# Four layers of attention and feed-forward on one core: attention and the feed-forward of the item two behind interleaved, the experts' outputs scaled by ScalarE and added by GpSimd

## The reference

```python
x = x + xattn0(ln(x))   # 16 heads of 8, key mask, 64 learned memory keys/values
x = x + ffn0(ln(x))     # 128 -> 512, exact GELU, -> 128, plus a rank-style term
                        # built from tokens 1..16 of each item, scaled
x = x + xattn1(ln(x))   # 16 heads, rms norm of q and k
x = x + ffn1(ln(x))     # 4 experts 128 -> 512 -> 128, silu(x@w1)*(x@w3) @ w2,
                        # the best 2 of each token weighted by the gates
x = x + xattn2(ln(x))   # 16 heads, rotary embedding
x = x + ffn2(ln(x))     # 8 experts (352 wide), top 2, plus a shared one (176)
x = x + xattn3(ln(x))   # one head of 128
x = x + ffn3(ln(x))     # top-2 weights of 7 gates times one matrix, plus shared
```

## Time and profile before

| | us |
|---|---|
| median of 3 runs | 1201.09 (1197.25 to 1201.25) |
| profiled execution: its own time | 1206.52 |
| its span | 1204.7 |
| busy: PE, PEld, DVE, ACT, POOL | 1005.4, 656.7, 552.0, 440.4, 261.5 |
| mean granted clock | 0.762 |

### The profile page before, as it was taken

One profiled execution on the slowest core, in us unless ns is written; L12 is line 12 of the kernel. 1 busy time (PEld: TensorE's weight loads), 2 busy tenths in 40 slices (PEclk: granted clock), 3 DMA queues, 4 the chain that ended last, 5 costly groups with the idle time before them and its releaser, 6 DMA issues. The chain is left out here.

```text
span 1204.7 us, 14263 instructions
## 1 busy us (share of the span) xinstructions
PE 1005.4 (83%) x5034; PEld 656.7 (55%) x5034; DVE 552.0 (46%) x1203; ACT 440.4 (37%) x649; POOL 261.5 (22%) x375
## 2 busy tenths in 40 slices
PE   3788777858658888779999788788789999999986
PEld 3534333225534444338888563433348888888874
DVE  2644453313344454424554544454434454534458
ACT  2344443332205434452343225444442332322240
POOL 7201032214314442211110104241110010101044
PEclk9666675567766555568999995655579999999997
DMA  5001010110001101110000002201210000000001
GB/s 126 2 1 19 1 19 2 18 18 16 1 0 54 37 1 36 36 18 9 1 1 1 1 13 64 43 14 35 40 21 5 1 1 1 1 1 1 1 1 35
DMA packets 24715, 21.01 MB, mean 17 GB/s; under 512 B 6559, under 2 KB 19847, under 8 KB 24519
## 3 DMA queue, kind: packets, MB, share of 16 engines
q1 hardware_dynamic: 24647, 20.10, 7.8%
HBM read 12.33 MB, written 1.05 MB: 11 GB/s over the span
## 5 line engine op out<-in xcount | busy, mean ns | idle before, releaser
L1134 DVE TENSOR_REDUCE mneg<-PS 128x4 f32<-128x624 f32 (+1 forms) x192 | 170.7, 894 | 180.5 <-PE PS L751 180.2
L1546 ACT ACTIVATE work<-PS 104x1024 f32<-104x1024 f32 (+1 forms) x160 | 163.5, 1022 | 182.4 <-PE PS L833 180.6
L1286 DVE TENSOR_TENSOR work<-PS,work 128x512 f32<-128x512 f32 (+2 forms) x168 | 114.8, 685 | 211.4 <-PE PS L885 134.9
L1576 ACT ACTIVATE work<-PS 128x512 f32<-128x512 f32 (+2 forms) x168 | 99.9, 597 | 243.5 <-PE PS L885 241.5
L902 PEld LDWEIGHTS PS<-down_w,work 128*128 128x128 f32 (+2 forms) x1472 | 175.4, 194 | 6.2 <-DVE work L1286 1.0
L902 PE MATMUL PS<-down_w,work 128*128 128x128 f32 (+2 forms) x1472 | 175.9, 277 | 0.7 <-DVE work L1286 0.7
L883 PE MATMUL PS<-xh_sb,arena 128*128 128x512 f32 (+2 forms) x352 | 152.6, 433 | 9.5 <-DVE work L1286 9.2
L848 PE MATMUL PS<-work,vb_sb 104*32 104x512 f32 (+1 forms) x640 | 147.6, 1014 | 3.4 <-ACT work L1546 3.4
L885 PE MATMUL PS<-xh_sb,arena 128*128 128x512 f32 (+2 forms) x352 | 142.8, 406 | 0.0
L884 PE MATMUL PS<-xl_sb,arena 128*128 128x512 f32 (+2 forms) x352 | 142.4, 405 | 0.0
L751 PE MATMUL PS<-kb_sb,qxt_sb 49*128 49x312 f32 x256 | 69.5, 530 | 57.9 <-DVE mneg L1134 52.7
(11 more groups left out here) (165 smaller groups left out, 1164.7 us busy)
## 6 DMA issues: line engine op xcount, KB each, us to landing
v_den<-raw_sb SPq DMA_DIRECT2D x24, 256.0 KB, 5.0
stage<-in_w SPq DMA_DIRECT2D x8, 256.0 KB, 5.2
stage<-in_wg SPq DMA_DIRECT2D x8, 176.0 KB, 2.5
stage<-in_wu SPq DMA_DIRECT2D x8, 176.0 KB, 2.5
x_res<-in_x SPq DMA_DIRECT2D x4, 256.0 KB, 4.9
down_w<-in_w SPq DMA_DIRECT2D x1, 1024.0 KB
down_w<-in_wd SPq DMA_DIRECT2D x8, 128.0 KB
out<-x_res SPq DMA_DIRECT2D x4, 256.0 KB, 2.3
```

What stands on the lines that cost most here:

```text
L1134: dve.tensor_reduce(to, PS[:, bank:bank + 2, 0:HB * head_width(layer)].rearrange("p f (n h) -> p f h n", h=HB), AX.X, ALU.max, negate=True ...
L1286: dve.tensor_tensor(HH[0:rows, e % 2, j, :], PS[0:rows, 2 * (n % 2) + 1, :], SS[0:rows, n % 2, :], ALU.mult).then_inc(*sig["h"].mark((i, n)))
L1546: act.activation(P[0:rows, m % P_RING, :, :], PS[0:rows, 0:2, :], ACT.Exp, scale=SCALE).then_inc(*sig["p"].mark((i, m)))
L1576: act.activation(SS[0:rows, n % 2, :], PS[0:rows, bank, :], ACT.Silu).then_inc(*sig["act"].mark((i, n)))
```

## The change

The items no longer run one after the other. The program is 15 steps. Step s does attention item s (0 to 11, layers 0 to 2) and feed-forward item s - 2, the one whose attention was done two steps before; from step 12 on layer 3 takes the place of attention. `step_pieces` gives each piece of a step a position, sorts them, and all engines walk the sorted list: PE does `st`, `pv`, `up`, `down`, ACT the exps, tanh and scaling, and so on. Rings for x are per kind, `work` holds only the probabilities and a new `hidden` the hidden features, so that both kinds can run at once. Weights of layer 2 go where those of layer 1 are no longer needed, expert by expert.

The PSUM banks are dealt out anew: scores 0 and 1; maxima, transposes and all small products 2 and 3; values 4 (so an attention item is done in two halves of its heads, each evacuated to `raw_sb` by itself); gate and up 5 and 6; down 7.

Silu is computed as x (1 + tanh(x/2)) / 2: ACT takes the tanh, DVE adds 1 and multiplies by the gate bank, and multiplies by the up bank and 0.5. The sum over experts changes for all but the last expert of an item: ACT copies the down bank with the gate as scale into `lora_tmp`, four times 128 x 128, and GpSimd adds it to x.

```diff
+N_ATT = 3 * B
+SKEW = 2
+N_STEPS = N_ATT + SKEW + 1
+BANK_MX, BANK_PV, BANK_UP, BANK_Y, BANK_F3 = 2, 4, 5, 7, 0
...
+def ffn_item(f):
+    return (f // B) * 8 + B + f % B
...
+def attention_pieces(a, put):
+
+    i = item_of(a)
+    N, C = n_slots(i), quads(i)
+    W = width(a)
+    scale = W / 29.0
+    for m in range(N // 2):
+        put(2 * m, "st", i, m)
+    for u in range(2 * C):
+        put(4 * u + 5, "pv", i, u)
+    put(4 * C + 2.5, "evac", i, 0)
+    put(N + 3, "evac", i, 1)
...
+def ffn_pieces(f, W, put):
+
+    i = ffn_item(f)
+    kind = ITEMS[i][0]
+    tiles = ffn_tiles(kind)
+    if kind == "F0":
+        for n in range(4):
+            put(1.7 + 2.2 * n, "up", i, n, 0)
+        put(W * 0.45, "down", i, 0)
+        put(W * 0.45 + 1, "acc", i, 0)
+        return
+    for n in range(len(tiles)):
+        put(W * (n + 0.3) / len(tiles), "up", i, n, 0)
+        put(W * (n + 0.55) / len(tiles), "silu", i, n)
+        put(W * (n + 0.8) / len(tiles), "up", i, n, 1)
+    for e in range(tiles[-1][0] + 1):
+        last = max(n for n, tl in enumerate(tiles) if tl[0] == e)
+        x = W * (last + 2.1) / len(tiles)
+        put(x, "down", i, e)
+        put(x + 0.3, "acc", i, e)
...
+def step_pieces(s):
+
+    placed = []
+
+    def put(x, *piece):
+        placed.append((x, len(placed), piece))
+
+    W = width(s)
...
+    if s < N_ATT:
+        attention_pieces(s, put)
+    if SKEW <= s < N_ATT + SKEW:
+        ffn_pieces(s - SKEW, W, put)
...
+    if s == 12:
+        attention3_pieces(0, 0.8, put)
+        ffn3_pieces(0, 23.6, 30.0, put)
+    if s == 13:
+        attention3_pieces(1, 0.8, put)
+        attention3_pieces(2, 9.0, put)
+        ffn3_pieces(1, 9.9, 17.0, put)
+        ffn3_pieces(2, 18.0, 25.0, put)
+    if s == 14:
+        attention3_pieces(3, 0.8, put)
+        ffn3_pieces(3, 9.0, 16.0, put)
...
+                bank = BANK_UP + (kt % 2 if kind == "F0" else 0)
...
+                taken[bank + m] = sig["h_gelu" if kind == "F0" else "h" if m else "silu"].at((i, kt))
...
+                taken[BANK_Y] = accumulated(i, e)
...
+            def silu(i, n):
+                rows = ffn_tiles(ITEMS[i][0])[n][2]
+                dve.wait_ge(*sig["act"].at((i, n)))
+                dve.scalar_tensor_tensor(SS[0:rows, n % 2, :], SS[0:rows, n % 2, :], 1.0, PS[0:rows, BANK_UP, :],
+                                         ALU.add, ALU.mult).then_inc(*sig["silu"].mark((i, n)))
...
-                    dve.tensor_tensor(HH[0:rows, e % 2, j, :], PS[0:rows, 2 * (n % 2) + 1, :], SS[0:rows, n % 2, :], ALU.mult).then_inc(*sig["h"].mark((i, n)))
...
+                dve.scalar_tensor_tensor(HH[0:rows, e % 2, j, :], SS[0:rows, n % 2, :], 0.5, PS[0:rows, BANK_UP + 1, :],
+                                         ALU.mult, ALU.mult).then_inc(*sig["h"].mark((i, n)))
...
+                if e < last_expert(kind):
+                    return
...
-                    act.activation(SS[0:rows, n % 2, :], PS[0:rows, bank, :], ACT.Silu).then_inc(*sig["act"].mark((i, n)))
...
+                    act.activation(SS[0:rows, n % 2, :], PS[0:rows, BANK_UP, :], ACT.Tanh, scale=0.5).then_inc(*sig["act"].mark((i, n)))
...
+            def gated(i, e):
+
+                if e < last_expert(ITEMS[i][0]):
+                    act.wait_ge(*sig["y"].at((i, e)))
+                    if e == 0:
+                        act.wait_ge(*sig["gates"].at(i))
+                    if e > 0:
+                        act.wait_ge(*sig["acc"].at((i, e - 1)))
+                    elif ITEMS[prev_item(i)][0] == "F0":
+                        act.wait_ge(*sig["lora_l"].at(prev_item(i)))
+                    else:
+                        act.wait_ge(*sig["acc"].at((prev_item(i), last_expert(ITEMS[prev_item(i)][0]) - 1)))
+                    for t in range(T):
+                        ins = act.activation(YG[:, t * 128:(t + 1) * 128], PS[:, BANK_Y, t * 128:(t + 1) * 128], ACT.Copy,
+                                             scale=gates[:, gate_slot(i), t, e:e + 1])
+                    ins.then_inc(*sig["gated"].mark((i, e)))
...
+            def accumulate(i, e):
+
+                if e < last_expert(ITEMS[i][0]):
+                    b = ITEMS[i][2]
+                    if e == 0:
+                        pool.wait_ge(*sig["xn"].at(i))
+                    else:
+                        pool.wait_ge(*sig["acc"].at((i, e - 1)))
+                    pool.wait_ge(*sig["gated"].at((i, e)))
+                    xb = x[:, b * T:(b + 1) * T, :]
+                    pool.tensor_tensor(xb, YG[:, :].rearrange("p (t n) -> p t n", t=T), xb, ALU.add).then_inc(*sig["acc"].mark((i, e)))
...
```

1058 lines of the change are left out of this document (523 added, 535 removed).

## The result

The changed kernel takes 1300.9 us (median, 1299.2 to 1306.5) beside 1199.2 of the kernel before in the same comparison: a ratio of 1.086 (95% interval 1.081 to 1.090). It is slower by 102 us where the forecast said 145 us faster; 1301 is outside the range of 985 to 1130.

What follows compares the result with a forecast made beforehand. Attention was taken as limited by PE at half clock, F1 and F2 by PE at full clock, F0 and the tail by waits. Step terms summed to a 1060 us span, 1056 us measured time; 8-in-10 range 985 to 1130.

Steps and rivals of the forecast that it cites:

- The clock: Steps 6 to 13: TensorE was taken to hold the upper level, 2.4 GHz; the forecast's condition.
- The paragraph on banks: Gate, up and small products on single pairs: use of 38 or 42 us lies under a step's 68.
- 0 to 12, I take 57: Steps 0 and 1, attention alone: A0's 52.8 us plus 0 to 12 for shared banks 2 and 3, taken as 57.
- The table loads in them: Steps 2 to 5: 32 loads of 1.28 us around Gelu, mostly hidden, 4 us a step exposed.
- The work: Steps 6 to 13: 512 us of busy time times clock, put at 616 us, a rate of 0.83.
- The 2.4 us: Gate bank's cycle: matmul to activation 0.97, activation 0.60, DVE operation 0.69, hand-off 0.1.
- The nearest row: Earlier trace, last F1 item mixed with A2's preparation: work share 0.82; the forecast took 0.85 for mixed steps.
- Steps 11 to 14: Last F2 items with the last attention and layer 3: 84, 82, 83 and 36 us.
- Gated sum, DMA: Expert sum on ACT and GpSimd: copies at 0.3 us, adds at 1.27, hidden; weight loads cost nothing, denominators' copy hidden.
- Bank hand-offs and a swinging clock: Rival for steps 6 to 13: rate 0.75, 683 us for 616, total 1123 us; chance 0.18.
- The slower rival: Clock drops in steps 6 to 13, mostly 1.2 GHz; rate 0.65, 788 us there, total 1228; chance 0.06.
- One sign of being wrong: Steps 2 to 5: the prediction is wrong if they exceed 75 us, where it had 66 and 60.

## Why the prediction was wrong

**The clock: right in its level, not free of loss.** It is 0.89 to 0.99 in steps 6 to 13, mostly the upper level, as the forecast took it. But it does not hold that level. Two stretches of 10 us in step 7:

```profile
600.00:610.00 10.00, 8.22 (x28) 4.26 (x29) 6.25 (x15) 4.57 (x7) 4.63 (x5) 0.66 0.00 1
660.00:670.00 10.00, 8.77 (x57) 6.36 (x55) 5.25 (x11) 3.65 (x8) 0.44 (x2) 1.00 0.01 2
```

28 matmuls in the one and 57 in the other, at about the same busy time. The Trainium skill's rule (TensorE: Matmul & The Clock Gate, "A second HAM failure mode: psum-queue depth-cycling"), which spoke against the forecast, says that idling between groups while cycling PSUM banks makes the clock swing; the trace agrees that it swings, between 0.66 and 1.00 here. Without the second DVE operation, with fewer waits for a bank, the same steps ran at 0.96; that the waits are what lowers the clock is the likely reading, not shown by itself. In steps 2 to 5 the clock stayed at 0.59 to 0.63 where I had let denser work raise it.

**The banks: the first step that failed.** The paragraph on banks named the right hand-overs and priced them too low, because it asked of each bank whether its total use fits into the step (42 under 68, 38 under 68). A bank's use is not spread over a step: TensorE takes its pieces in a fixed order, and each piece whose bank is not back yet stops all behind it. For the small products I had "0 to 12, I take 57" in steps 0 and 1 and nothing later; the kernel before with that sharing alone loses 81 us, 4 to 15 us an item, and the steps 0 and 1 measured 62.8 and 71.4. Step 1 also holds the preparation of the first F0 item, which the sum had only in later steps. For steps 2 to 5 I take the same sharing and the lower clock to be most of the 70 us; no run shows it with interleaving, but without it a second pair for the reductions took 34 us off these four steps. The table loads in them (4 a step, the 1.28 us of the earlier trace rows) were sized right.

**The work: a term that was too small.** The forecast counts work as busy time times clock. In that count the 746 us of steps 6 to 13, for which it had 616, are about 596 of work, 37 that PE was busy longer because the clock was below 1.00, and 113 of idle PE. The forecast had 512 of work and 104 for everything else. So 84 of the 130 us are work and 46 are waits and clock. Some 49 of the 84 stood in the earlier trace rows: the same pieces are 561 us there by stage (half of A1 42, F1 166, A2 77.5, F2 247, three quarters of the tail 28), while the sum built F1 from 16 tiles an item (146 for the stage's 166) and F2 likewise (238 for 247), which leaves out the preparations for later items that stand in these stages, and took too little for the last layers. The other 35 were not tried apart; the first matmul of a gate or up group took 504 ns in the mean after 433, and the "work" of step 7 is about 67 us with and without the second DVE operation.

**Gate and up: cycle right, its effect too small.** The 2.4 us came out at 2.39. But 16 x 2.4 = 38 us "under 68" was no cover in the mixed steps: without the second DVE operation steps 7 and 8 fall by 7 us. The nearest row, 0.82 in the earlier trace rows, from which I went up to 0.85, came from a stretch in which gate and up had two pairs; I named that in the rival and not in the term. In the forecast's own measure (512 us over the measured 746) the rate came out at 0.69; with the work as it was it is 0.80, so more of that miss is the work than the waits.

**Steps 11 to 14.** 329.5 for 285. The F2 tile of 2.97 us (8.9 for an expert) is 3.4 to 4.1 in the mean of a step. Tiles 2.35 us apart, as forecast, are there, but the one behind which a down projection stands is mostly 4.1 to 5.9 us from the next where the forecast had 4.1. The last layers' chains stand in the same order as the tiles; TensorE waits 7 us for their layer norm in steps 11 to 13 and 35 for DVE's operations on tiles. The second pair and Silu together gave back 16 us. Step 14 was 41 for 36, at a clock of 0.55, where the tail before had 0.83.

**Gated sum, DMA.** The copy took 0.372 us for a guess of 0.3, the addition 1.285 for 1.27; with the sum back on DVE the time was the same. DVE's wait for the denominators' copy fell from 84 to 4 us, so that term, hidden, was right.

**The rivals.** "Bank hand-offs and a swinging clock" had the mechanism, both halves of it, and stopped at a rate of 0.75 and at step 6; it gave 1123. The slower rival came nearest in number (1228) by a mechanism that did not occur, the lower level in most of steps 6 to 13. One sign of being wrong that the forecast named did come: steps 2 to 5 exceed 75 us, all four. A case with bank hand-offs in all steps, attention's included, was missing; the range was too narrow by it.

## What to carry to other kernels

Before interleaving two streams on an in-order engine, count the banks that each of them gives up for it, and price each lost double buffer alone, by putting just that loss into the kernel before: here the three losses (small products on one pair, gate and up on one pair, the second DVE operation) cost 81 + 164 = 245 us in the kernel before, and interleaving gained 191. A bank's total use was no guide here; ask for each matmul what was last written to its bank and how long ago. A second buffer helps only if it is free: one taken from other pieces moved the wait to them (ratio 0.997), and only with banks freed in F0's stage as well did the old kernel gain 1.7%. And when work is added up for a new order, start from the busy time of whole stages: a sum built from the main pieces alone left out 49 us here.

## What the runs showed of the hardware

Short waits can cost TensorE twice. Step 0 with its 196 matmuls ran 62.8 us at a granted clock of 0.55 with waits for the reduction, and 42.8 us at 0.86 with a second pair of banks: 15.6 of the 20 us are busy time for the same work, and with it the clock. The other traces with one pair and with two repeat it (60.0 to 63.2 and 41.1 us). It need not follow: the next step lost 9 us of idle time too and stayed at 0.60. That fewer waits raised the clock in step 0 is the likely reading; no run moved the clock alone. A single added DVE operation of 0.68 us a tile cost 35 us with DVE busy 67 to 72% of the stages, although 16 table loads of ScalarE went with it.
